# Order of two steps on TensorE and ScalarE, the place of a late product, the output scales and the head of a load queue in a fused WKV and binary FFN kernel

## The reference

```python
tf = sigmoid(sum(cond, -1))                                 # one per batch
decay = exp(-exp(w)) * (0.5 + 0.5 * tf)                     # batch x channel
ek = exp(minimum(k, 30)); ekv = ek * k
nf, df = forward scans  a = a * decay + ekv, b = b * decay + ek
nb, db = the same scans backwards in time
euk = exp(minimum(u + k, 30))
num = nf + nb - ekv + euk * k
den = df + db - ek + euk
y = sigmoid(x) * num / maximum(den, 1e-8) * (0.8 + 0.2 * tf)
bw = where(weight >= 0, 1, -1) * mean(abs(weight), axis=1)
out = x + (y @ bw.T + bias)
```

## Time and profile before

| | value |
|---|---|
| median of 3 runs | 526.22 us (525.59 to 526.37) |
| profiled execution | 526.13 us |
| its span | 524.3 us |
| VectorE busy | 494.6 us, 94% of the span |
| TensorE, ScalarE, GpSimd busy | 365.8, 392.5, 370.3 us |
| granted TensorE clock, mean | 0.856 of full |

### The profile page before, as it was taken

How to read it: one execution, slowest core, us unless ns; L and a number is a source line. 1 busy time by engine, 2 the same in 40 slices (tenths; PEclk the granted TensorE clock), 3 DMA queues, 4 the chain that set the end, 5 groups by cost and what they waited for, 6 DMA issues and landing times.

```text
span 524.3 us, 5375 instructions
## 1 busy us (share of the span) xinstructions
PE 365.8 (70%) x1797; PEld 212.0 (40%) x1803; DVE 494.6 (94%) x376; ACT 392.5 (75%) x435; POOL 370.3 (71%) x202
## 2 busy tenths in 40 slices
PE   2333322333588787787887796979567999889993
PEld 2222212222254444444444453545235555544441
DVE  5999999999999999999999999999999999999854
ACT  2869889797849999999969889696865787674400
POOL 0068777768787777778778877778877689887122
PEclk9999965555597797889889797999877999999998
DMA  7776999999987998887788999597654679775198
GB/s 212 190 228 216 257 236 266 278 292 257 256 219 181 202 200 158 167 157 177 184 186 176 201 201 190 94 200 175 146 105 75 115 123 146 103 100 81 30 154 137
DMA packets 100835, 92.65 MB, mean 177 GB/s; under 512 B 2860, under 2 KB 93000, under 8 KB 100296
## 3 DMA queue, kind: packets, MB, share of 16 engines
q0 software_dynamic: 32016, 37.75, 47.5%
q1 hardware_dynamic: 66712, 53.50, 32.4%
q10 hardware_dynamic: 2080, 1.05, 0.7%
HBM read 58.74 MB, written 37.75 MB: 184 GB/s over the span
## 4 chain that ended last, share of the span: by engine, by line
DVE 68%; issue 20%; PE 7%; ACT 2%; POOL 1%; DMA 0%; DVEq 0%; SPq 0%; POOLq 0%; ACTq 0%
DVE pair L827 25%; DVE pair L841 14%; DVE pair L853 7%; DVE wkv L870 7%; DVE own L854 6%; DVE pair L850 4%; PE sT L445 2%; DVE euk L876 2%; PE prod L404 1%; PE prod L445 1%; PE kT L445 1%; DVE y_start L833 1%; PE kT L379 1%; PE cols L445 0%; DMA cond<-in_cond_dram 0%
## 5 line engine op out<-in xcount | busy, mean ns | idle before, releaser
L404 PE MATMUL prod<-acts,sgn 128*128 128x512 f16 x752 | 191.4, 413 | 3.9 <-ACT orow L737 3.1
L841 DVE TENSOR_TENSOR_SCAN pair<-cols,y_start,pair 128x1024 f32<-128x1024 f32 x64 | 150.1, 2346 | 1.3 <-DVE y_start L833 0.2
L827 DVE TENSOR_TENSOR_SCAN pair<-cols,pair 128x1024 f32<-128x1024 f32 x64 | 142.9, 2274 | 0.0
L404 PEld LDWEIGHTS prod<-acts,sgn 128*128 128x128 f16 x752 | 79.4, 106 | 98.6 <-issue 27.2
L345 POOL TENSOR_TENSOR wkv<-wkv,rec 128x1024 f32<-128x1024 f32 x31 | 73.4, 2368 | 38.9 <-ACT wkv L682 38.6
L336 POOL TENSOR_TENSOR wkv<-euk,rec 128x1024 f32<-128x1024 f32 x31 | 78.6, 2536 | 24.7 <-ACT rec L639 24.7
L379 PE MATMUL kT<-ident,k_nat 128*128 128x128 f32 x256 | 47.0, 345 | 65.8 <-DVE own L854 65.8
L356 POOL TENSOR_TENSOR wkv<-wkv,pair 128x1024 f32<-128x1024 f32 x31 | 73.5, 2369 | 10.8 <-DVE wkv L870 10.5
L303 POOL TENSOR_TENSOR acts<-wkv,rec 128x1024 f16<-128x1024 f32 x30 | 71.4, 2380 | 0.0
L379 PEld LDWEIGHTS kT<-ident,k_nat 128*128 128x128 f32 x256 | 38.7, 180 | 73.4 <-issue 72.4
L637 ACT ACTIVATE rec<-euk,lnb 128x1024 f32<-128x1024 f32 x31 | 35.6, 1149 | 42.9 <-DVE euk L876 42.9
(11 more groups left out here) (110 smaller groups left out, 534.1 us busy)
## 6 DMA issues: line engine op xcount, KB each, us to landing
pair<-own POOLq DMA_DIRECT2D x32, 512.0 KB, 4.6
out_dram<-in_x_dram SPq DMA_DIRECT2D x32, 512.0 KB, 6.3
k_nat<-in_fside_BxSxS_dram SPq DMA_DIRECT2D x30, 512.0 KB, 4.7
x_nat<-in_x_dram SPq DMA_DIRECT2D x26, 512.0 KB, 6.2
out_dram<-o_nat POOLq DMA_DIRECT2D x24, 512.0 KB, 6.3
y_fm<-in_L_ffn_weight_dram SPq DMA_DIRECT2D x8, 512.0 KB, 6.8
out_dram<-in_L_ffn_bias_dram POOLq DMA_DIRECT2D x8, 512.0 KB, 8.8
x_end<-in_x_dram SPq DMA_DIRECT2D x6, 512.0 KB, 7.1
```

What stands on the lines that cost most here:

```text
L404: ins = pe.matmul(made_in(u), view[:, c, m % CT * P:m % CT * P + P], acts[:, part, m // CT % 2 * CT + c, h * H:(h + 1) * H], start=(part = ...
L827: dve.tensor_tensor_scan(buf, d, buf, 0.0, ALU.mult, ALU.add).then_inc(st["F" + kind], 1)
L841: dve.tensor_tensor_scan(buf[:, ::-1], d, buf[:, ::-1], y_start[:, i:i + 1], ALU.mult, ALU.add)\
```

## The change

The diff has five parts. The order of TensorE: turned(34) leaves the end of step 25 and stands in step 26 behind k_turn(27). The order of ScalarE in step 26: y_copy(33) goes ahead of halves, and evac(35) with y_copy(34) go behind two. The end: the 12 matmuls of across(6) go ahead of the wait for the low halves (`prior_lo`, `last_lo`) and ahead of ended(0) to ended(4). The output scales: VectorE's L861 in step 8 becomes four ScalarE activations of 128 x 8 with a scale per partition, behind halves and ahead of two. The start: the sync queue begins with k tile 0, and ScalarE's queue loads cond; on VectorE the copy of the decays to PSUM moves behind three links, and two small operations (back_ps and gain) go behind the first L850.

```diff
@@ @block.sync
+            sp.dma_start(k_nat[0][:, :, :], tile_of(k, 0)).then_inc(k_in[0], 16)
             for i, a in enumerate((w, u, bias)):
                 sp.dma_start(rows[i * CT:(i + 1) * CT, :], a.rearrange("(c p) -> c p", p=P)).then_inc(s_par, 16)
-            sp.dma_start(cond4[:, :], cond).then_inc(s_cond, 16)
             sp.wait_ge(s_par, 48)
@@ @block.tensor
                     turned(units[0])
                     unit(units[3])
                     turned(units[1])
-                    turned(units[2])
                     units = ()
+                if n == LAST + 2:
+                    turned(units[0] - 2)
                 for u in units[0:1]:
                     turned(u - 1)
...
             across(5, bank[5], range(CT - 2), True, False)
+            pe.wait_ge(st["last_gate"], 1)
+            across(6, bank[6], range(CT - 2), True, False)
...
-            pe.wait_ge(st["last_gate"], 1)
             pe.wait_ge(st["prior_lo"], 1)
             pe.wait_ge(st["last_lo"], 1)
-            for v in range(3):
-                ended(v, CT - 2)
-            across(6, bank[6], range(CT - 2), True, False)
-            for v in range(3, 5):
+            for v in range(5):
                 ended(v, CT - 2)
             pe.wait_ge(st["last_gate"], 2)
@@ @block.scalar
-            act.dma_start(k_nat[0][:, :, :], tile_of(k, 0)).then_inc(k_in[0], 16)
+            act.dma_start(cond4[:, :], cond).then_inc(s_cond, 16)
...
+                if n == LAST + 2:
+                    y_copy(4 * CT + 1)
...
                     halves(n - 2, p)
-                sooner = min(made(n - 1), cleared(n - 1) + 1)
+                sooner = cleared(n - 1) if n == LAST + 2 else min(made(n - 1), cleared(n - 1) + 1)
+                if not wt and not late:
+
+                    done(act, "abs", CT - 1)
+                    act.wait_ge(s_gain, 1)
+                    for b in range(B):
+                        ins = act.activation(oscale[:, b * CT:(b + 1) * CT], asum[:, :], ACT.Identity,
+                                             scale=gain[:, b:b + 1])
+                    ins.then_inc(s_osc, 1)
                 if n == LAST:
                     y_copy(4 * CT - 1)
-                if n == LAST + 2:
-                    y_copy(4 * CT + 1)
@@ @block.vector
-            link(dve.tensor_copy(dec_ps, dec[:, :]))
             link(dve.tensor_scalar(onem[:, :], dec[:, :], -1.0, 1.0, ALU.mult, ALU.add))
             link(dve.scalar_tensor_tensor(scl[:, :], dec[:, :], 1.0, onem[:, :], ALU.add, ALU.mult))
             link(dve.tensor_scalar(scl[:, :], scl[:, :], S_MIN, None, ALU.max))
+            link(dve.tensor_copy(dec_ps, dec[:, :]))
             link(dve.reciprocal(back[:, :], scl[:, :]))
-            link(dve.tensor_tensor(back_ps, back[:, :], dec[:, :], ALU.mult))
-            link(dve.tensor_scalar(gain[:, :], tf[:, :], 0.2 / HI_SCALE / (C * SIGN), 0.8 / HI_SCALE / (C * SIGN),
-                                   ALU.mult, ALU.add))
+
+            def shares():
+
+                link(dve.tensor_tensor(back_ps, back[:, :], dec[:, :], ALU.mult))
+                dve.tensor_scalar(gain[:, :], tf[:, :], 0.2 / HI_SCALE / (C * SIGN), 0.8 / HI_SCALE / (C * SIGN),
+                                  ALU.mult, ALU.add).then_inc(s_gain, 1)
...
                 dve.tensor_scalar(E, E, E30, scl[:, n:n + 1], ALU.min, ALU.mult).then_inc(st["clamp"], 1)
+                if n == 0:
+                    shares()
...
-                if not wt and not late:
-
-                    done(dve, "abs", CT - 1)
-                    dve.tensor_tensor(oscale[:, :].rearrange("p (b c) -> p b c", b=B), per_batch(asum[:, :]),
-                                      gain[:, :].unsqueeze(2).to_broadcast([P, B, CT]), ALU.mult).then_inc(s_osc, 1)
-
                 starts(n, p)
```

More of the change, by code:

```diff
@@ L157, in bi_wkv_binary_ffn @@
         csum_ps = prod[:, 1, 0:B]
-        s_par, s_cond, s_id, s_rows, s_wub, s_csum, s_every, s_ew, s_eew, s_ecs, s_const, s_ucol, s_dve, s_osc = (
+        s_par, s_cond, s_id, s_rows, s_wub, s_csum, s_every, s_ew, s_eew, s_ecs, s_const, s_ucol, s_dve, s_osc, s_gain = (
             sem(a) for a in ("s_par", "s_cond", "s_id", "s_rows", "s_wub", "s_csum", "s_every", "s_ew", "s_eew", "s_ecs",
-                             "s_const", "s_ucol", "s_dve", "s_osc"))
+                             "s_const", "s_ucol", "s_dve", "s_osc", "s_gain"))
         k_in, w_in, num_in = ([sem(f"{a}{p}") for p in range(2)] for a in ("k_in", "w_in", "num_in"))
```

## The result

The changed kernel takes 521.1 us (520.72 to 521.59, 6 runs) where the kernel before takes 525.9 us (524.63 to 526.79, 6 runs): a ratio of 0.9909, 95% interval 0.9895 to 0.9924, so 4.8 us less. The forecast was 521.7 us, 4.55 us less. The profiled execution spans 519.5 us against 524.3 us.

A forecast was written before the change was run, and what follows sets the result against it. VectorE was taken to bound the kernel, held up by late GpSimd in steps 26 and 27. Terms -3.07 - 0.73 - 1.0 + 0.25 = -4.55 us took the median 526.22 to 521.7 us, range 520.8 to 523.6.

The forecast's parts named there:

- What bounds: VectorE, 68% of the chain of waits; steps 26 and 27 together 3.07 us above two clean steps of 14.70.
- The two marks: Steps 26 and 27: L870 late for GpSimd's L345; L876 2.17 long instead of 1.23, waiting for L356's SBUF port.
- Steps 25 and 26: Reordering TensorE and ScalarE there makes GpSimd early: steps 26 and 27 give back 3.07 us, bounds 3.1 and 1.7.
- rival D: TensorE stays at its lower clock through step 26; unit(37) ends later than about 409; slower, 527.7 us; chance 0.03.
- Rival A: Steps 26 and 27 come back only in part, ScalarE being the new last one; 523.0 us; chance 0.12.
- B: Steps 26 and 27: L876's excess is its own and stays; 523.6 us; chance 0.03.
- Output scales: Step 8: L861 waits for the port; moving it to ScalarE gives -0.73 us, bounds -0.75 and -0.1.
- The end: across(6) fills TensorE's hole ahead of ended(0), last pieces come earlier: -1.0 us, bounds -1.05 and -0.5.
- The start: Loads reordered, small operations behind the first L850: rows held behind k, +0.25 us, bounds -0.85 and +0.9.
- the 8.8 to 8.9 named as a sign: Step 0: L850, the first operation, was to stand at 8.8 to 8.9 us; beyond 9.6 the prediction is wrong.
- Rival C: Start: rows land at 5.5 or more, 0.9 late, 522.5 us; or gains of 0.85, 520.7; chance 0.12 together.
- The sum: Whole kernel: -3.07 - 0.73 - 1.0 + 0.25 = -4.55 us, giving 521.7 us from the median of 526.22.

The follow-up runs named there:

- the kernel with fills: Changed kernel plus GpSimd write-only operations: one, two, three ahead of L356 in steps 10, 12, 14; two, three behind it in 15, 16; 525.98 us.

## Why the prediction was right, point by point

**What bounds.** Right. The two marks in steps 26 and 27 were the cost, and both were VectorE waiting for GpSimd, once at a semaphore and once at the port. The second half was an inference from one distance, 406.29 to 407.30, and the kernel with fills has shown it. The prediction puts no time of step 27 down to the clock, and there is some: behind the idle of 5.22, turned(34), s_turn(25) and unit(36) take 1.09, 1.92 and 4.34, and in the changed kernel 0.60, 1.04 and 3.62, some 2.1 less.

**Steps 25 and 26.** Forecast 3.07, measured 3.05. The steps of the sum hold to 0.1 or 0.2 when counted from the step's first operation: two at +5.03 forecast, +5.05 measured; GpSimd's wait ahead of L345 1.3 forecast, 1.26 measured; unit(37) done by 402.8 forecast, turned(36) behind it at 402.64 measured. TensorE idled 1.03 ahead of turned(35), about half of my 2, and its granted clock stayed at 1.00. Its timeline in the changed kernel:

```profile
398.72 0.63 PE L379 MATMUL yT<-ident,y_fm 128*128 128x128 f32 x4 [1.03 <-ACT o_nat L624]
```

Its four transposes took 0.63, against 1.09 behind the idle of 5.22. So rival D (slower, by a lower clock) did not come, and its condition, unit(37) later than 409, was 6 us away. Its sum has a slip in words: the 3.07 are taken off because its 6.0 count from a clean step, not because they are gained, and the terms make 527.6. Rival A (the two steps come back in part) did not come, since both are clean, and B (an excess of L876's own) is out by two experiments. What I had in the wrong order of weight is seen only in the single parts: ScalarE's order gives 2.34 alone and TensorE's 1.75.

**Output scales.** Step 8: forecast 0.73, measured 0.74. The four activations took 0.86 for my 0.8, and two moved 0.23 for my 0.36. That the 1.02 of L861 held a wait for GpSimd's L345 rests on the earlier trace rows and on the same picture in the kernel that puts it back, where L865 is 1.02 long again; no run gave L861 a free port. Not foreseen: the stall of 0.21 in step 29 became one of 0.36 in step 20, and the 0.22 in step 23 went.

**The end.** Forecast 1.0, measured 1.01 and 1.02; ended(0) was to start 1.6 later and starts 1.57 later.

**The start.** The sum gave +0.25, the first operation came 0.46 late in the profile (0.18 to 0.22 in three other executions with these loads), inside the bounds, but not at the 8.8 to 8.9 named as a sign: it stood at 9.22, and at 8.94 to 8.98 in the three others. Two terms of the sum were off and cancelled in part. shares() was to cost 0.15 and costs nothing: from the first operation to L865 1.02 pass, before 1.01. The rows were to land at 4.7 and landed at 5.37, in the three others at 5.09 to 5.13. The reason I gave, order on one queue, was not the one that the runs support. The rule of the Trainium skill, page "DMA: Bandwidth & Descriptors", section "Queues, rings and completion order", order within one ring, may hold, but it does not set the time here: on another queue the rows were as late. One reading was too strong as well: that the landed k did not bind k_turn(0). In the kernel before k is issued at 1.68 and lands 3.8 later, at 5.48, and k_turn(0) starts at 5.50, when the product ends. The two came together, so an earlier k alone could gain nothing. Rival C (rows at 5.5 or later) came near, at 5.37, but not in.

**The sum.** 4.55 forecast, 4.8 measured; the steps named make up 4.35 of it, and 0.07 from the steps 20, 23 and 29 and 0.36 of scatter at the end are what was not in the sum. That the total came so near is in part luck: the scatter at the end made up for the 0.21 that the start cost beyond its term.

## What to carry to other kernels

When the bound engine's timeline has longer instructions and no idle, look at what GpSimd runs beside them: an operation with two SBUF inputs is stretched for as long as GpSimd reads, and the cure is to start GpSimd's operation earlier, that is, to find the wait at the head of its chain. Ask in each late step which work stands ahead of the instruction that another engine waits for, and move that work behind it; the longest idle in the trace need not be it. Small loads on which the start depends are issued ahead of the first large one, not behind it: here that was worth 0.53 us. An idle of TensorE can cost more than its length, since the matmuls behind it may run at the lower granted clock.

## What was not expected of the hardware

A fill of 128x512 on GpSimd, 0.53 us long, held a 0.74 us tensor_scalar for 0.43 but not a two-input operation that ran beside it. A small load issued 0.24 us after a 512 KB load on the other queue took 2.47 us, where one issued ahead of it needed 1.5 to 1.7. Moving one small operation from VectorE to ScalarE turned a stall of 0.21 in step 29 into one of 0.37 in step 20, the same in every execution. The same order of work on TensorE left unit(36) at 4.34 us in one execution and 4.95 in another, by how soon the granted clock rose again after an idle.
